# A four-layer attention kernel on one core: new step orders for every engine, and PSUM banks dealt from a table

## The reference, cut to what matters

```python
x = _L0_cond_ref(x, cond_1024[:, None, :], ...)   # adaptive layernorm, 16 heads of 64, MLP with exact gelu
x = _L1_cond_ref(x, cond_1024, ...)               # RMS norm with FiLM, one head of 128, MLP
x = _L2_cond_ref(x, cond_1024, ...)               # adaptive layernorm, 16 heads of 8, MLP
x = _L3_cond_ref(x, cond_1024, mask_BxSxSx11_ik0, ...)   # graph attention, 16 heads, 20 keys, labels per edge
return x
```

## Time and profile before

| what | value |
|---|---|
| median of three runs | 1163.77 us (1160.85 to 1166.27) |
| span of the profiled execution | 1164.6 us |
| its time outside the span | the page shows none; the span is taken as its time |
| instructions | 24661 |
| TensorE busy | 1080.4 us, 93% |
| VectorE busy | 894.3 us, 77% |
| ScalarE busy | 807.3 us, 69% |
| GpSimd busy | 446.9 us, 38% |

### The profile page before, as it was taken

How to read it: one execution, slowest core, us unless ns; L and a number is a source line. 1 busy time by engine, 2 the same in 40 slices (tenths; PEclk the granted TensorE clock), 3 DMA queues, 4 the chain that set the end, 5 groups by cost and what they waited for, 6 DMA issues and landing times.

```text
span 1164.6 us, 24661 instructions
## 1 busy us (share of the span) xinstructions
PE 1080.4 (93%) x8525; PEld 752.7 (65%) x8525; DVE 894.3 (77%) x2623; ACT 807.3 (69%) x2956; POOL 446.9 (38%) x632
## 2 busy tenths in 40 slices
PE   5999999999999999999999999999999888887774
PEld 4667767666776676667675667667775666564452
DVE  2666768778787898788977898778877975885865
ACT  1667677778967678767875786777875875684461
POOL 2232324224433354235532445334522641441532
PEclk9999999999999999999999999999899999979886
DMA  7000000100010000100000000100010001000000
GB/s 238 11 2 19 1 1 19 32 9 11 2 33 6 10 10 1 32 19 11 1 8 26 19 6 2 32 20 1 1 42 5 2 2 41 1 2 25 1 2 14
DMA packets 21889, 21.02 MB, mean 18 GB/s; under 512 B 1207, under 2 KB 20360, under 8 KB 21512
## 3 DMA queue, kind: packets, MB, share of 16 engines
q1 hardware_dynamic: 18600, 15.26, 4.5%
q10 hardware_dynamic: 3168, 4.19, 1.2%
HBM read 17.35 MB, written 2.10 MB: 17 GB/s over the span
## 4 chain that ended last, share of the span: by engine, by line
PE 64%; DVE 18%; ACT 13%; issue 2%; POOL 2%; DMA 1%; SPq 0%; POOLq 0%; DVEq 0%; ACTq 0%
PE bank L1033 11%; PE bank L1041 7%; PE bank L1053 6%; PE bank L1079 5%; ACT prob_space L963 5%; PE bank L1094 4%; PE bank L1058 4%; PE bank L1104 4%; PE bank L1088 4%; PE bank L1162 3%; PE bank L1170 3%; PE bank L1027 3%; ACT fprobs L899 2%; PE bank L1180 2%; PE bank L1255 2%
## 5 line engine op out<-in xcount | busy, mean ns | idle before, releaser
L786 POOL TENSOR_TENSOR fprobs<-fprobs,frinv 128x512 f32<-128x512 f32 (+1 forms) x144 | 136.1, 950 | 253.3 <-DVE frinv L1351 252.1
L899 ACT ACTIVATE fprobs<-bank,fnegmax 128x128 f32<-128x128 f32 x512 | 181.4, 381 | 54.3 <-DVE fnegmax L1346 53.8
L963 ACT ACTIVATE prob_space<-bank,negmax 128x128 f32<-128x128 f32 x512 | 182.0, 386 | 31.8 <-DVE negmax L1478 31.7
L1033 PE MATMUL bank<-fhT,w_qkv 128*128 128x512 f32 (+1 forms) x288 | 125.5, 559 | 0.3 <-DVE fhT L1321 0.3
L1346 DVE TENSOR_REDUCE fnegmax<-bank 128x4 f32<-128x512 f32 (+1 forms) x144 | 83.9, 624 | 44.8 <-PE bank L1079 43.9
L963 ACT ACTIVATION_READ_ACCUMULATOR prob_space<-bank,negmax 128x1 f32 x512 | 114.8, 226 | 0.0
L899 ACT ACTIVATION_READ_ACCUMULATOR fprobs<-bank,fnegmax 128x1 f32 x512 | 111.8, 219 | 0.0
L759 POOL TENSOR_TENSOR rstd<-veps,half 128x4 f32<-128x4 f32 (+1 forms) x45 | 42.4, 943 | 148.8 <-DVE veps L1308 112.6
L905 ACT ACTIVATE fprobsT<-bank 128x512 f32<-128x512 f32 (+1 forms) x144 | 76.5, 557 | 28.8 <-PE bank L1088 28.5
L1478 DVE TENSOR_REDUCE negmax<-bank 128x4 f32<-128x512 f32 x128 | 82.0, 682 | 12.4 <-PE bank L1162 11.9
L1170 PE MATMUL bank<-ident,prob_space 128*128 128x128 f32 x512 | 81.5, 293 | 9.9 <-ACT prob_space L963 9.1
(11 more groups left out here) (192 smaller groups left out, 2567.0 us busy)
## 6 DMA issues: line engine op xcount, KB each, us to landing
adj<-in_mask_BxSxSx_ik SPq DMA_DIRECT2D x32, 110.0 KB
adj<-in_mask_BxSxSx_ik SPq DMA_DIRECT2D x7, 440.0 KB
x_norm<-in_x SPq DMA_DIRECT2D x7, 256.0 KB, 2.9
x_res<-in_x SPq DMA_DIRECT2D x7, 256.0 KB, 2.9
out<-x_out SPq DMA_DIRECT2D x7, 256.0 KB, 2.4
w_qkv<-in_L_cond_W_qkv ACTq DMA_DIRECT2D x1, 1536.0 KB, 7.5
prob_space<-in_w_mod SPq DMA_DIRECT2D x1, 1024.0 KB
w_up<-in_w_up ACTq DMA_DIRECT2D x1, 768.0 KB, 10.1
```

Source lines behind the costliest of these rows:

```text
L786: pool.tensor_tensor(p, p, wide(frinv[:, u, 0:P.n], D), ALU.mult).then_inc(fnormed.sem, 1)
L899: ins = act.activation(fprobs[:, u % NP, b, :], P.bank(("S", u))[:, tok(b)], ACT.Exp, bias=fnegmax[:, u, b:b + 1], accum_out=frsum[:, u, b ...
L963: ins = act.activation(probs[:, u % NP, i, :], P.bank(("A", u))[:, tok(i)], ACT.Exp, bias=negmax[:, u, i:i + 1], accum_out=rsum[:, u, i:i ...
L1033: ins = pe.matmul(P.result(result), w, a[:, 0:P.t], start=(i == 0), stop=(i == len(terms) - 1))
```

## The change

The step lists, the instructions of each step and the waits are those of before. Three things differ.

All four strings in `ORDERS` are others: the same letters the same number of times, in another order.

A bank is no longer dealt by the rule of the longest free. `BANKS` is a string of 1419 digits, one for each result in the order in which TensorE begins them, and `Plan` takes the next digit.

The check on it is looser: a bank may be dealt again once TensorE's order is past the step that wrote its former result (for a result that one step writes whole, a later result of the same step may take it). The second scores of a pair and the scores of layer 1 now count as ended in the step that writes them, where before they ended at "E", "E2", "E1" or the next "u3". The wait for the drain on the chip stays.

```diff
-                            "S": ([("S", 2 * c), ("S", 2 * c + 1)], [("S", 2 * c)]),
-                            "E": ([], [("S", 2 * c + 1)]),
+                            "S": ([("S", 2 * c), ("S", 2 * c + 1)], [("S", 2 * c), ("S", 2 * c + 1)]),
+                            "E": ([], []),
...
-               Step("E1", 0, [], ["A1"]), Step("T1", 0, ["T1"], ["T1"]), Step("a1", 0, ["a1"], ["a1"]),
+               Step("E1", 0, [], []), Step("T1", 0, ["T1"], ["T1"]), Step("a1", 0, ["a1"], ["a1"]),
...
-            begins, ends = {"S2": ([("A", 2 * w), ("A", 2 * w + 1)], [("A", 2 * w)]),
-                            "E2": ([], [("A", 2 * w + 1)]),
+            begins, ends = {"S2": ([("A", 2 * w), ("A", 2 * w + 1)], [("A", 2 * w), ("A", 2 * w + 1)]),
+                            "E2": ([], []),
...
-            ends.append(("S3", s))
+            ends += [("S3", s), ("S3", s + 1)] if s % 2 == 0 else []
...
 class Plan:
-    def __init__(self, banks, orders, prefer):
+    def __init__(self, banks, orders, deals):
...
-        free_from = {b: i - 100 for i, b in enumerate(prefer)}
+        written = [-1] * 8
...
+        deal = iter(deals)
         for p, x in enumerate(order):
             for r in STEPS[x][went[x]].begins:
-                b = min(free_from, key=lambda b: free_from[b])
-                assert free_from[b] < p, (p, x, r)
-                free_from[b] = ends[x, r]
+                b = int(next(deal))
+                assert written[b] < p, (p, x, r)
+                written[b] = ends[x, r] - (ends[x, r] == p)
                 self.at[x, r] = (b, dealt[b])
...
-        plan = Plan(banks, ORDERS["all"], prefer=(0, 1, 4, 5, 6, 7, 2, 3))
+        plan = Plan(banks, ORDERS["all"], "".join(BANKS.split()))
```

More of the change, by code:

```diff
@@ L110, in mid_steps @@
     return (mlp_steps(0) + norm_steps(2)
[L111 to L112 removed]
+            + [Step("qk1", 0, ["q1", "k1"], ["q1", "k1"]), Step("v1", 0, ["v1"], ["v1"]), Step("A1", 0, ["A1"], ["A1"]),
+               Step("E1", 0, [], []), Step("T1", 0, ["T1"], ["T1"]), Step("a1", 0, ["a1"], ["a1"]),
                Step("o1", 0, ["o1"], ["o1"])]
@@ L192 @@
[L192 to L201, removed]
@@ new lines @@
+            "AAAAAAAAAAAAAAAAAAAAAAAAAAAAAAAAAAAAAAAAAAAAAAAAAAAAAAAAAAAAAAAAABBBBAAAABBBBAAABBBAABBBABBABJBBBJBJBBBBBBBBBB"
+            "BBBBBBBBBBBBBBBBBBBBBBBBBBBBBBJJBBBJJCJBJCJCBJBBCJCCJBJBCBJCJBJCCJBBCCJCJJCCBJJCCCCCBJCCCCCJCCCCCCKKSKCKKCCSCK"
+            "SCKCCCCKCKCCCCCCCCCCCCCCCCCCKKCCSCSCCSSKCKCKCSSSCCCCKKCSSDSKCSKDSSSCSSKSKDSDKSDCSKKSDDDSSKKDDCSLDSSDDDDSLSDDDS"
+            "DSDLDTDTDLLDDDDLTLDbDDLTLLDTDDDDDLDTTTDDDDDLTLDLTDDDLTDLDDTDTLDDDTLLLDTTTDDTTTbLDDDDTTbDLLbDDTTbDDTDDTbDDTTDDD"
@@ new lines @@
+            "hIIIIIZIhZIZZhRZZZhZZZhRZhZZRZZRRZhhZZRRhZZRZZhRZZhZZRZZZRRZZRhRZRZZRZRRRZZhZRZRhZRZRZhRZhZZZZZZhRiiiiaaaiaaii"
+            "aaaaaaaaaiaiaiaiaaaaiaiaiaaaaiaiiaaiaaajjjjjjjjjjjjjj"
+        ),
+        "DVE": (
+            "AAAAAAAAAAAAAAAAAAAAAAAAAAAAAAAAAAAAAAAAAAAAAAAAAAAAAAAAAAAAAAAAAABBBBAAABBABBAABBBAABBABBBABJBBJBBBBBBBBBBBBB"
+            "BBBBJBBBBBBBBBBBJBBBBBBBBBBBBBBBBJBJJJJJCBCBJBCCBJBJCJJJCCCBBBCCJJBJBJCCJCCJJBCCCJCCJCCCCBCKCCCKKCCCCKCCKCSSKC"
+            "KCCCCCCKSCCCCCCCCCCCCCKCCKCCCCCKCCSCSSCKCKKSCCCKKSSSSSCCCKSSSKDKSSSCDKSSSCDSKDCDSSDDKSSDDDSSDKSDSDCDDDKKLDLDDL"
+            "SDDLLSDSDTDDTDLTDLDbDLDDLTLDTDDDLTTTDDDDDDLLLDDLTDDDDTDTLDTDDLTDTLLTTTDDLTTDLDDbDTLTDTDbLDDDTbbDDDDDTTTTTbTDTD"
+            "TTDDDbbbTEETTLDTTDTbTETETEEEbTbETETEETTTETbEDELbMEMTEEEEETEEMTEEUUEEMMMUMEEcUUEEEMUEUUUMEcEEEMUEEEEUEEMEEcEMcE"
+            "UUUMEEMcMEEEEccUEMEEcEEEUUEUEUEUEUUEMEUcEUEEcEFMUUEMUUEMEEUUEUMcUcFUUMUEcUUcUEMFUFUcUFFcUFEFUUUUFFFFUFFMFUUMcN"
+            "NcFUUNFFFFFFNFFVVFVFFFNFdFFNNVFFdFVNFNVVFVFVFFFFdVFVNVFFFFNVFFNNVdNNFVVVVFVVddFFFFFFFFVFFFNFVFNVdFdFVFNNFFFVVG"
+            "NVVdVVFFFVVNdFVGGdGNGdGVNVVVGGVVVFGddGFVNGGdVdGGVVGFVVGGNGGVGddVVOVGGGOVGOGWOOGOGGGWGOGGWOGGOGOWWOGGWWeWOeOGGW"
+            "WeWOGGWOeGGGWWGeGGWWGWWGWOGWOGWOWGWGGOGGWeOGGWWGWGWeGGGGWGOWGGWWHeHeGWeWeWOeGWGWGGOOWHWeWHeWeGGWHHHWWGWGWWHOHH"
+            "eWHWePPHHPHWWXeHHXHPHPHXPHHXfHHHPHHXHHHHXHXPHPXXHHHPHHHHHHfHHPHfXHXPXXPXfHHXXXHHPHXXffXPPHHHHXfXXHXfPXXHHXHHXH"
+            "HXPPXHXfPXHHPHfHIHXHffHPIXXfXfXXHHIHfIHIfIXPXIXHIPIIXIfIXIXIIIIXHXXIfPIHQXIXQXIQIQIIQXIYIgQYQYgQgQIIYIYIIgIIIY"
+            "IIQYYYgIYIQYYYQYYgQQgQYYQYYYgIIIIYYYgYgYYYIYQYYYQQIYIYgIgQYYIIYIYYQIYgIYgYgYgIIIYYYYQIYYIIIgYIIQQQIIIYgYIIIZIh"
+            "IIIZIZhIhZIRZZhRZZZZZhZZZZhhRZRhRZZhZZRRhZZRZRZhZZZRZZZZRhRRZZRRZZhZZZZRRhRZRRZRhRZZZZZRRZRZhhhZZZiiiaiaaiaaia"
+            "aaiaiaaaaaiaiaaaaiaaiaiiaaiiaaaaaaaiiaajjjjjjjjjjjjjj"
+        ),
@@ new lines @@
+BANKS = """
+01456723014563721045763120465371204675120467152460712540761245067124506715264057126470153264703125470314270314
+62073416203741620347162073410634761324031472364207316420763410527634107532416075320156732501673201632507136250
+71326517205361573260510712630573056721053217063075463207564120356315423607154236540271354026713250673157316205
+37612301236017260726135602163507126715673201537201752035206175260531206735235017625702541765072451604750264724
+56021345602713641264513453423065472305604567420576240627405603250327650376240732564072356407306425702506754230
@@ new lines @@
+76450256403246032546037245607425316253076450346257035406371240372156042317504316273652073162057136205672105267
+10360531067351026753126325713256731602376120732517623052763510371531205731205705136270167530751364730457105346
+37214062750361475236231062147036217403217640321307214072630172361704237642034702362403640274136026701274162076
+42763427634267142626071271246262426047610247150742163542163074156273071362416753240167245041504165401760410657
+41726412764012570517625104627541541602547021547064726520615042674125046176102407416056172054706514067245017425
@@ L254, in step_at @@
+03416253425073651407640237602673501256732567031705271056205136207156273120713527153061271506513205320675123073
+57610261306257625701632706153206715320617320654713204671534061254702635412635127543601425360743260251736502436
+741526370451263704512604375126403751264035126734516072350164732156730412567304126537042615370426153
+"""
 def step_at(letter, what, n=0):
@@ L332, in __init__ @@
             went[x] += 1
+        assert next(deal, None) is None
     def view(self, letter, g):
```

88 lines of the change are left out of this document (38 added, 50 removed).

## The result

The changed kernel takes 1136.53 us (1135.69 to 1137.73, four runs) against 1164.99 for the kernel before in runs on the same chips: ratio 0.9756 [0.9731, 0.9782], 28 us less.

What follows compares the result with a forecast made beforehand. It took TensorE as the limit up to 883 us, then one chain's exponentials, maxima and small steps. Terms +5 - 7.5 - 3 - 2.5 = -8, with 0.8 more off 1164.6, gave 1156 us; own range 1146 to 1158, whole 1145 to 1172.

Steps and rivals of the forecast that it cites:

- banks: Bank reuse, 100 to 883 us: 62 more tight places leave less margin for queued drains; +5 us, bounds 0 and +31.
- look-ahead in the long stretch: 21 to 883 us: more TensorE work between a result and its use absorbs late neighbours; -7.5 us, bounds 0 and -15.
- Y's and Z's backs: 883 to 1075 us: shorter TensorE waits for exponentials and copied probabilities; net -3 us, bounds -6 and +3.
- a's back: 1075 to 1136 us: "turn4" ahead of u3(0) brings the first "S2" earlier; -2.5 us, bounds 0 and -5.
- What bounds the kernel: TensorE limits up to 883 us, where an order wins at most its 15 us idle; afterwards one chain's small steps.
- The ruler: TensorE's orders laid out with each step's traced matmul time plus 0.05 us to the next; both fill 1048 us.
- shortfalls: How far TensorE's work between steps misses the shortest latencies in the last groups: 9.4 us before, 5.2 after.
- Nothing comes of it: Rival: waits up to 883 us are queueing, so look-ahead gives nothing; 1163 us, chance 0.33.
- Late drains: Rival: drains stand behind other work at the new tight places, bank term +21; 1172 us, chance 0.20.
- The clock: Rival: short bank waits lower TensorE's clock in the long stretch to 0.97, costing 23 us; 1179 us, chance 0.03.
- What would show it: Right: long stretch no idler, shorter late waits, earlier "S2"; wrong: over 15 us of new drain waits, among others.

Runs made afterwards that it cites:

- x1: The changed kernel's orders with each result dealt the bank drained longest ago in that kernel's trace: 1135.04 us, ratio 0.9722 to the kernel before.
- x2: The orders of the kernel before, with each result dealt the bank drained longest ago in that kernel's trace: 1161.64 us, ratio 0.9963 to it.
- x12: Old orders up to TensorE's step 1418, new ones from there, banks dealt as in x2: 1158.96 us, ratio 0.9957 to the kernel before.
- x5: x1 with 53 neighbouring pairs swapped in TensorE's string, positions 133 to 1103, for 347 tiling changes instead of 291: 1169.39 us.
- x10: x1 with 113 extra useless matmuls ahead of TensorE's 41 long waits from position 1103 on: 1125.97 us, ratio 0.9669 to the kernel before.

## Why the prediction was off, step by step

| term of the sum | forecast | shown |
|---|---|---|
| banks | +5 | some +1.5 against roomy banks (after against x1), within the noise; those of before cost 4 (before against x2) |
| look-ahead in the long stretch | -7.5, no more than the idle 15 | -9.4, of it -13.1 inside "busy" and +3.4 of waits |
| Y's and Z's backs | -3 (-6 to +3) | -18.9 (1103 to 1382): 13.3 waits, 5.0 in the steps |
| a's back | -2.5 | -2.1 in x12, -2.4 in the changed kernel |

Two steps failed: the rule that TensorE can win no more than its idle time, and the size of the term for Y's and Z's backs, which holds most of the missing 20 us.

*What bounds the kernel* failed at one sentence: that an order can win in the long stretch "no more than the 15 us that it idles". It took the page's idle time for the whole of what lies between steps. The two windows from 101 to 819.6 us have 9 us of idle time by the page, and 45 us of gaps by the steps. The ruler then gave every boundary the same 0.05 us, which hid the one difference that mattered there: 0.00 between full-array steps, 0.095 at a change of tiling. The longer distances that I expected to swallow waits did not do so in the trace: the waits over 0.15 us grew by 3.4 us, and with roomy banks on both sides by 6.4 (10.7 in x2, 17.1 in x1), so it was not the banks. That the look-ahead term of -7.5 came near -9.4 is luck.

*Y's and Z's backs*: the term was too small by a factor of five to six. (The forecast's stretch began at 883 us. Cut nearer to it, from 860.2 to 1074.8 us before and with the same steps from 847.4 to 1047.6 after, it is 14.4 us shorter; the 3.4 won from 819.6 to 860.2 belong to the first stretch.) The longer waits between 1103 and 1382, sorted by the step that waits, show what was mis-sized:

| waiting step | before | after | x2 | x1 |
|---|---|---|---|---|
| "T2", "T2'", "V2" | 11.6 | 5.9 | 11.2 | 6.1 |
| steps of the end streams | 3.8 | 1.0 | 3.9 | 0.9 |
| "S2" | 3.3 | 1.4 | 4.9 | 1.7 |
| all others | 11.5 | 8.6 | 10.1 | 9.3 |

The places that the prediction named came out as it said: shortfalls that fall by 4.2 (9.4 to 5.2), waits that fall by 5.7. For the end streams it had 1.5 us more, and they lost 2.8. Of "S2" and the rest it had nothing. The shortfalls were added up with the shortest latencies seen, as if each engine stood ready. But VectorE was 86% busy in Y's back, and with the new order its idle time there fell from 12.8 to 6.3 us, which no ruler on TensorE's work alone shows. That a late VectorE was the cause of these waits is my reading; no run changed VectorE's string alone. The lost clock was not priced as something to win either; 0.97 and 0.90 stood in the earlier trace rows.

*The banks*: right in that nearly all tight pairs still leave time, wrong in the +5. The table of the old rule cost the old orders some 4 us itself (before against x2). *a's back*: right in its place, its mechanism and its size (2.8 us up to the first "S2", where 2.4 were forecast).

*The rivals.* "Nothing comes of it" fell by its time, but its point held: in the long stretch the longer distances swallowed no waits, and what was won there is of another kind. "Late drains" fell with x1. "The clock" did not come: 1.00 in the long stretch, as before. The rule cited there (the Trainium skill, "TensorE: Matmul & The Clock Gate", section "A second HAM failure mode: psum-queue depth-cycling") is not shown by this kernel with tight banks either; x5's fall stood behind one wait of 2.66 us.

*What would show it.* Shorter waits of the backs and a shorter way to a's first "S2" came; the idle share of the long stretch rose slightly (11.3 to 13.7 us), and yet the time fell. In 100 to 815 us the rows of waits have 0.4 us on fattnT and 0.3 on fprobsT drains, far from the 15 that would have shown it wrong.

What stays open is which engine's string brings the second gain. The four strings of that part were made for each other; single ones were not tried.

## What to carry to other kernels

Before you take an engine's idle time for the ceiling of what an order can win, look inside its busy time: go from step to step and list the gaps by the kinds of the two neighbours. Put TensorE's steps that use a part of its array next to each other, best those on the same strips, if the data are there in time. Look at the second busiest engine of a stretch too: where the backs won most, VectorE's idle time halved, though which of the two caused the other was not tried apart. And compare with a control that has everything else of the change: x2 and x1 told orders from banks, and showed the shorter waits again but not the 5 us of clock. Here a clock that fell in waits was worth less than (1 - clock) x length, and a little idle work inside long waits fetched it back (x10).

## What was not expected of the hardware

- A change between a full-array matmul and one on 64 or 32 rows or columns costs 0.095 us ahead of the step and up to 0.10 us in the full-array step behind it ("o": 0.96 against 0.86 us); two "S2" on strips of 32 rows take 1.60 us together, one alone 1.06.
- The clock can be bought back, but returns less than it seems to: in the tail it rose from 0.84 (x1) to 0.97 (x10), 16 us of lost clock by (1 - clock) x length, and the tail got 3.1 us shorter (119.6 to 116.5; the other traces with the new orders there and no extra matmuls take 117.8 to 121.1). In the stretch before, 5.0 us of lost clock (0.94 over 82.6) gave back 4.8 (77.8).
